# Two-layer GNN with expert FFNs: second FFN product per expert in node order, gate weights applied to its sums

## The reference, cut to what matters

```python
x = x + gnn0(ln(x))   # mean over edges of feat[src] * w, next to feat itself, @ W.T + b
x = x + ffn0(ln(x))   # 8 experts, 256 -> 512 -> 256, relu
x = x + gnn1(ln(x))   # h = relu(x @ Wp.T + bp); h @ W1.T + sqrt(sum over edges of w * h[src]**2) @ W2.T
x = x + ffn1(ln(x))   # 8 experts, 256 -> 256 -> 256, gelu, plus its own input
# both ffn: for every token the two best experts by gate, weights comb[token, e] (0 for the others)
h = act(tokens @ W1[e] + b1[e]); y = h @ W2[e] + b2[e]
out += comb[:, e:e+1] * y        # over all 8 experts
```

## Time and profile before

| | |
|---|---|
| median of 3 runs | 3251.39 us (3250.32 to 3257.69) |
| the profiled execution | 3246.49 us, its span 3244.1 us |
| PE, DVE, ACT, POOL busy | 76%, 55%, 35%, 52% of the span |
| granted PE clock, mean | 0.894 of full speed |
| layer 0, full tile with gathers (tile 8) | 129.9 us |
| layer 1, full tile with gathers (tile 8) | 101.5 us |

### The profile page before, as it was taken

One profiled execution on the slowest core, in us unless ns is written; L12 is line 12 of the kernel. 1 busy time (PEld: TensorE's weight loads), 2 busy tenths in 40 slices (PEclk: granted clock), 3 DMA queues, 4 the chain that ended last, 5 costly groups with the idle time before them and its releaser, 6 DMA issues.

```text
span 3244.1 us, 47395 instructions
## 1 busy us (share of the span) xinstructions
PE 2453.5 (76%) x17987; PEld 1405.7 (43%) x17987; DVE 1779.2 (55%) x4298; ACT 1133.1 (35%) x1835; POOL 1681.3 (52%) x1678
## 2 busy tenths in 40 slices
PE   0136889989989989899999623478787777877897
PEld 0123444544444445444457522344443444444455
DVE  8454666656566566565666433244454544545565
ACT  3022333343343433333545401133232333333455
POOL 3666545454464554544330166566666666666520
PEclk9998999999999999999999855588787888888899
DMA  5532223232232322322220212112212222122110
GB/s 205 202 89 85 80 86 90 81 92 75 85 90 80 92 83 81 89 82 78 68 58 18 81 47 54 41 54 61 59 51 55 62 60 62 51 55 60 50 36 9
DMA packets 115789, 238.02 MB, mean 73 GB/s; under 512 B 30290, under 2 KB 69452, under 8 KB 115044
## 3 DMA queue, kind: packets, MB, share of 16 engines
q0 software_dynamic: 66560, 163.68, 18.2%
q1 hardware_dynamic: 48996, 71.26, 6.4%
HBM read 209.16 MB, written 25.67 MB: 72 GB/s over the span
## 4 chain that ended last, share of the span: by engine, by line
PE 45%; DVE 19%; another core or an unknown queue 16%; issue 12%; ACT 6%; DMA 1%; POOL 1%; DVEq 0%; ACTq 0%; SPq 0%; POOLq 0%
PE psY L714 16%; PE psH L684 14%; DVE hid L1271 4%; PE psM L778 4%; PE psE L674 4%; DVE hsc L1276 3%; PE psE L666 3%; ACT hid L1459 2%; PE psC L691 1%; DVE acc L1110 1%; ACT hsc L1466 1%; DVE wbuf L1022 1%; PE psM L730 1%; DVE mag L968 1%
## 5 line engine op out<-in xcount | busy, mean ns | idle before, releaser
L591 POOL DMA_INDIRECT ring<-table,src_s x1664 | 1653.2, 993 | 1364.3 <-issue 624.9
L714 PE MATMUL psY<-hsc,wbuf 128*128 128x512 f16 (+2 forms) x4032 | 945.3, 371 | 231.7 <-DVE hsc L1276 91.7
L684 PE MATMUL psH<-xnT,wbuf 128*128 128x512 f16 (+2 forms) x4032 | 932.2, 369 | 40.4 <-ACT hid L1459 26.1
L1459 ACT ACTIVATE hid<-psH,b,scl 128x512 f32<-128x512 f32 (+2 forms) x672 | 485.8, 723 | 1289.8 <-PE psH L684 778.5
L1271 DVE TENSOR_TENSOR hid<-hid,psC 128x512 f32<-128x512 f32 (+2 forms) x672 | 415.9, 619 | 573.2 <-ACT hid L1459 408.7
L714 PEld LDWEIGHTS psY<-hsc,wbuf 128*128 128x128 f16 x4032 | 365.2, 101 | 725.6 <-DVE hsc L1276 187.5
L684 PEld LDWEIGHTS psH<-xnT,wbuf 128*128 128x128 f16 x4032 | 383.8, 104 | 373.1 <-issue 79.5
L1110 DVE TENSOR_TENSOR acc<-acc,psE 128x120 f32 (+1 forms) x416 | 98.5, 237 | 656.2 <-remote 477.5
L1276 DVE TENSOR_TENSOR hsc<-hid,hsc 128x512 f16<-128x512 f32 (+2 forms) x672 | 416.3, 619 | 0.4 <-ACT hsc L1466 0.4
L1466 ACT ACTIVATE hsc<-hid 128x512 f16<-128x512 f32 (+2 forms) x672 | 380.1, 566 | 2.9 <-DVE hid L1271 1.9
L674 PEld LDWEIGHTS psE<-ohbuf,ring 128*128 128x128 f32 x1664 | 263.6, 232 | 55.3 <-DMA ring<-table,src_s 22.5
(11 more groups left out here) (155 smaller groups left out, 1764.8 us busy)
## 6 DMA issues: line engine op xcount, KB each, us to landing
ring<-table,src_s POOLq DMA_INDIRECT x1664
wbuf<-w_in SPq DMA_DIRECT2D x2, 4096.0 KB, 16.0
wbuf<-x_in SPq DMA_DIRECT2D x7, 896.0 KB, 11.5
table<-ring SPq DMA_DIRECT2D x7, 896.0 KB, 3.6
feat<-table SPq DMA_DIRECT2D x11, 512.0 KB
xin<-x_in SPq DMA_DIRECT2D x11, 512.0 KB
x_d<-x SPq DMA_DIRECT2D x11, 512.0 KB
xin<-x_d SPq DMA_DIRECT2D x11, 512.0 KB
```

Of the source, the lines that this page charges most:

```text
L591: pool.indirect_dma_start(out=l.ring[:, g % l.R, k, :], out_offset=None, in_=l.table, in_offset=bass.IndirectOffsetOnAxis(ap=src_s[:, c:c ...
L684: last = mm(psH[n % 2][:, 0:l.TT[t]], l.w1(e, i, k, c), x[:, j, k, 0:l.TT[t]], start=(k == 0 and m == 0), stop=(k == KD - 1 and m == 2))
L714: last = mm(psY[d][:, 0:l.TT[t]], l.w2(e, i, c, d), hsc[n % 2][:, j, 0:l.TT[t]], start=False, stop=(n == l.M - 1 and m == 2))
L1459: f(hid[n % 4][:, 0:l.TT[t]], psH[n % 2][:, 0:l.TT[t]], (ACT.Relu, ACT.Gelu)[l.i], scale=l.un_up, bias=l.b1[:, n // l.HC, n % l.HC:n % l.H ...
```

## The change

`down` now takes 128 nodes of the hidden tile as the stationary operand and a 128 x 256 piece of the second matrix as the moving one, so that psY holds nodes by features, four blocks in two banks, for one expert at a time. The bias of the expert comes first, as a product with a matrix that has ones in row e (`spread[:, e, :]`), 24 x 128 by 24 x 256. After an expert's last chunk DVE multiplies each block with its gate weight and adds it to `res`, which is the result at the end of the tile (`weighted`; three `res` tiles in place of two and x2). `scale`, `spread_weights`, `back_to_tokens`, the cut, transposed and copied weights, `sum_copied`, yT, x2 and bank psC are gone. psE has two banks, one for even and one for odd groups; PE may start a group when the one before the last has been added, and DVE adds each group when it alone is summed. In layer 0 the node counts of a group are summed ahead of the wait for its gather. The order by step changes in layer 1 (take, linear, norm, gate at 4, 6, 10, 12; groups from step 5 on, over 15 steps), and the end of `gate_weights` runs in the first steps of the tile that it is for. `t0nb` is made by four operations of one column.

```diff
-                self.at_take, self.at_lin, self.at_norm, self.at_gate, self.at_comb = (
-                    (13, 18, 22, 24, 29), (1, 3, 7, 9, 13))[i]
+                self.at_take, self.at_lin, self.at_norm, self.at_gate = (
+                    (13, 18, 22, 24), (4, 6, 10, 12))[i]
...
-                self.turn = (18, 1)[i]
+                self.turn = (18, 5)[i]
...
+            def window(self, g):
+                o = g % self.OB // 2 * self.parts * W
+                return psE[g % 2][:, o:o + self.parts * W]
...
+            def y(self, s):
+                return psY[s // 2][:, s % 2 * D:(s % 2 + 1) * D]
...
+            def added(self, t, e, b):
+                return NX * self.CB[t] + e * self.NB[t] + b + 1
...
-                    if gs[0]:
-                        pe.wait_ge(l.window_added, gs[0])
+                    if gs[0] > 1:
+                        pe.wait_ge(l.window_added, gs[0] - 1)
...
             def down(l, t, n):
...
+                e, c, b = n // l.HC, n % l.HC, l.BT[t]
+                x, gs = hsc[n % 2], l.at(t, n)
+                if c == 0:
+                    for s in range(b):
+                        if s % 2 == 0 and (e or t):
+                            pe.wait_ge(l.y_added, l.added(t, e - 1, s // 2) if e else NX * l.CB[t])
+                        mm(l.y(s), spread[:, e, :], b2s[l.i][:, :], start=(s % 2 == 0), stop=False)
+                for s in range(b):
+                    v = slice(s * P, (s + 1) * P)
+                    for j in range(2):
+                        if s == 0 and j == 0:
+                            pe.wait_ge(l.hid_hi, l.M * t + n + 1)
+                        if s == 0 and j == 1 and l.i == 1 and n == l.at_lin and t < l.NT - 1:
+                            pe.wait_ge(l.logits_taken, t + 1)
+                        if s == b - 1 and j == 1 and gs and gs[0] > 1:
+                            pe.wait_ge(l.window_added, gs[0] - 1)
+                        mm(l.y(s), x[:, 0, v], l.w2(e, j, c), start=False, stop=False)
+                for s in range(b):
+                    v = slice(s * P, (s + 1) * P)
+                    if s == 0:
+                        pe.wait_ge(l.hid_lo, l.M * t + n + 1)
+                    if s == b - 1 and gs and l.i == 1:
+                        pe.wait_ge(l.onehot_ready, gs[-1] + 1)
+                    last = mm(l.y(s), x[:, 1, v], l.w2(e, 0, c), start=False,
+                              stop=(c == l.HC - 1 and (s % 2 == 1 or s == b - 1)))
                 last.then_inc(l.hid_used, 1)
...
-                dve.scalar_tensor_tensor(t0nb[:, v], t0mv[:, v, 0], -1.0, t0rs[:, v], ALU.mult, ALU.mult)\
-                   .then_inc(s_t0r, 1)
+                for j in range(i * XR, i * XR + XA):
+                    last = ts_(t0nb[:, j:j + 1], t0mv[:, j, 0:1], t0rs[:, j:j + 1], -1.0, ALU.mult, ALU.mult)
+                last.then_inc(s_t0r, 1)
...
-                    dve.wait_ge(l.group_summed, gs[-1] + 1)
+                    dve.wait_ge(l.group_summed, g + 1)
...
+            def weighted(l, t, e):
+                dve.wait_ge(l.hid_used, l.M * t + (e + 1) * l.HC)
+                for b in range(l.NB[t]):
+                    if e:
+                        dve.wait_ge(l.y_added, l.added(t, e - 1, b))
+                    for s in range(2 * b, min(2 * b + 2, l.BT[t])):
+                        r = res[t % 3][:, s, :]
+                        last = dve.scalar_tensor_tensor(r, l.y(s), comb[t % 2][:, s, e:e + 1], r, ALU.mult, ALU.add)
+                    last.then_inc(l.y_added, 1)
...
                     for n in range(l.M):
-                        if n + 1 < l.M:
-                            scale(l, t, n + 1)
-                        elif not last:
-                            scale(l, t + 1, 0)
                         hidden_low(l, t, n)
+                        if n == l.HC:
+                            for _ in weighing:
+                                pass
+                        if n and n % l.HC == 0:
+                            weighted(l, t, n // l.HC - 1)
+                        if n == 0 and t:
+                            result(l, t - 1)
                         add_windows(l, l.at(t, n - 1))
                         onehots(l, l.at(t, n + 1))
```

More of the change, by code:

```diff
@@ L191, in build_program @@
         featT = sb("featT", [P, KD, T])
-        res = [sb(f"res{i}", [P, SUB, D]) for i in range(2)]
+        res = [sb(f"res{i}", [P, SUB, D]) for i in range(3)]
         xn = sb("xn", [P, SUB, D])
@@ L795, in logits @@
                 last.then_inc(l.logits_summed, 1)
-            def weights_transposed(l, u):
-                pe.wait_ge(l.comb_split, u + 1)
-                for s in range(l.BT[u]):
-                    last = pe.transpose(cps[0:CP * NX, s, :], c72[:, s, :], ident_b[:, :])
-                last.then_inc(l.combT_summed, 1)
             for l in L:
@@ L1279, in result @@
-            def result(l, tt):
-                wait(dve, l.out_stored, 16 * tt)
-                for b in range(l.NB[tt]):
-                    dve.wait_ge(l.ytok_summed, l.CB[tt] + b + 1)
-                    v = slice(2 * b, min(2 * b + 2, l.BT[tt]))
-                    tt_(x2[:, v, :], res[tt % 2][:, v, :],
-                        psM[b][:, 0:(v.stop - v.start) * D].rearrange("p (s d) -> p s d", d=D), ALU.add)\
-                        .then_inc(l.out_ready, 1)
+                v = slice(0, l.TT[t])
```

222 lines of the change are left out of this document (69 added, 153 removed).

## The result

| | before | after |
|---|---|---|
| median of 4 runs | 3254.3 us | 3369.6 us (3358.6 to 3380.9) |
| ratio | 1 | 1.036, 95% interval 1.033 to 1.039 |
| span of the profiled execution | 3244.1 us | 3356.8 us |
| layer 0, tiles 8 and 10 | 129.9, 103.2 us | 135.4, 114.3 us |
| layer 1, tiles 8 and 10 | 101.5, 55.7 us | 107.6, 72.5 us |

What follows compares the result with a forecast made beforehand. Layer 0 was taken as PE-bound, layer 1 as a mixture of POOL's gathers and holes. Terms -11 + 16 - 65 - 125 - 12 + 34 + 25 = -138, with 15 held back -123, gave 3128 us, range 3070 to 3190.

Steps and rivals of the forecast that it cites:

- front: Stage ahead of the gathers: four one-column `t0nb` operations end ACT's 13.1 us of waits, passed on whole, -11 us.
- PE's own work: PE in both layers: more second and bias products, less spreading and transposing, +16 us, all on PE's path.
- layer 0 waits: PE's waits in layer 0 for low half, gate weights and spread ones: -55, with clock -10, together -65 us.
- layer 1 waits: PE's waits in layer 1 for gate weights, window sums, low half, spreading product: -110, with the clock -125 us.
- the 15 held back: 15 us kept off the predicted gain for work that moves to tile starts, where gate weights' operations queue on DVE.
- heads and tails: First and last tiles of each layer: gate weights, copies and transposes leave the path, -3 and -3 per layer, -12 us.
- drain: PE waits at each expert's bias product until DVE takes the last sums from psY: +34 layer 0, +25 layer 1.
- Waits that go: Step on PE's waits, heads and tails: shorter chain before the second product, 1.4 us before 2.6 of cover; -65, -125, -12.
- Layer 1 doesn't move: Rival, 0.14: 13.75 us hole stays, gather ring fills behind it, only front and layer 0 count: 3202 us.
- My bound of 181 us: Layer 1: POOL stood 181 us waiting for others than itself; more than that can't be gained there.
- The drain of psY decides, and it is slower: Rival, 0.15: at each expert's first bias product PE loses 1.2 us, 235 us in place of 59: 3304 us.
- loads don't hide: Rival, 0.05: second product's stationary slices of `hsc` load visibly, 0.02 us for each of 3024 more, +60: 3188 us.

Runs made afterwards that it cites:

- late batch: Runs on one chip in one stretch of time, in which the kernel before took 3250 to 3260 us.
- split alone: Kernel before with only the small operation of the first layer norm (`t0nb`) split: 2843.5 against 2846.3 us, ratio 0.999.
- three banks: Changed kernel, psY given the group sums' bank, DVE draining first, PE bank by bank, norm behind drain: 2830.0 us (0.996) prompt, 3266.3 us (1.002) late.
- prompt batches: Runs on one chip in one stretch of time, in which the kernel before took 2841 to 2846 us.
- no drain: Changed kernel, but PE waits for psY and DVE takes it only once a tile: 3235.5 us (0.992) late, 2835.4 us (0.998) prompt.
- b0: Kernel before, unedited and profiled, in a late batch: 3265.9 us.
- b1: Kernel before, unedited, run for its trace in a prompt batch: 2845.1 us.
- the stops: POOL waits until rows land, every group in layer 0, every fourth in layer 1: kernel before 3190.0 us (1.121), three banks 3169.8 us (1.113), prompt.

## Why the prediction was wrong, point by point

The terms against what the runs give, for a late batch, us:

| term | predicted | measured | from |
|---|---|---|---|
| front | -11 | -3 | split alone |
| PE's own work | +16 | about as said | layer 0 tile 113.5 before, 114.6 with three banks, in prompt batches; 0.8 predicted |
| layer 0 waits | -65 | about -26 | an estimate: tiles 1 to 8 take 131.6 before, 129.8 without the drain; 0.8 of own work added back, by ten tiles |
| layer 1 waits | -125 | none | tiles 1 to 8: 102.5 before, 103.9 without the drain |
| all but the drain, after the 15 held back | -182 | -24 | no drain, 0.992 |
| heads and tails | -12 | about -23 | layer 0's last tile and the stage behind it 291.1 to 265.0, layer 1's tile 0 97.3 to 100.1, which also holds the groups moved into it |
| drain | +59 | +161 | changed kernel less no drain, same batch |

"Before" in the tile rows is b0, from the other late batch. -24 and +161 make the +137 us of their batch by the way they were measured; the rows above the -24 are estimates and leave some 12 us of it open.

**The step that failed first is "Waits that go", above all its -125 for layer 1.** It took the listed reasons as the causes, and booked each wait of PE as a gain once its operation was shorter or nearer. The operations were seldom too slow to hide: in a prompt batch, with the same durations (activation 0.78 us, high copy 0.62, low half 0.69), the kernel before loses 14.0 us to the low half in layer 0 where a late one loses 40 to 46. What makes the rest of the holes in a late batch is that ACT, DVE and POOL get PE's updates late, 134 times by 2.0 us in the mean for ACT alone, and the new order's 1.2 us of slack (2.6 of cover for 1.4 of chain) doesn't cover that: without the drain PE stands 45.5 us in layer 0 for the two halves, where I had left 5 for them. Layer 1 tiles are 102.5 us before, 103.9 without the drain, 100 to 108 with three banks, and POOL stands there as long as before (185 us against 181). The 25 us for less time at 1.2 GHz went the other way, too: the mean granted clock fell from 0.894 to 0.877 without the drain. *Layer 1 doesn't move* was right about layer 1, at 0.14; its own reason, one long hole behind which the ring fills, is not what these traces show. The page of the profile had the hint: 16% of the chain that ended last was put down to another core or an unknown queue, and of POOL's stand in layer 1 the largest part beside its own issue time, 129.7 us, was "remote". My bound of 181 us from that row took it for waits that PE could shorten.

**The second is the price of the drain**, 161 instead of 59. *The drain of psY decides, and it is slower* had the mechanism, at 0.15, and a time of 3304, too low because the other terms weren't there; its 1.2 us a boundary is near the dearer ones without a norm (1.15), but the cost isn't spread as it said: half of what a layer 0 tile loses undisturbed is one boundary.
Three things were off. First the times behind a boundary without a group, 0.75 us predicted and 1.35 in the one shown. There the high copy ends 0.28 us behind the old products where I had 0.1 (it takes 0.71 us with its scale from memory where the row said 0.62), the low half takes 0.75 instead of 0.69, DVE's four operations follow each other 0.39 apart instead of 0.35 and start later, so that the second bank is taken at 2.76 us instead of 2.3, and the next products start 0.1 us behind the last bias product. Second, a group between the products pays for less than I had, and more seldom: 0, 0.4 and 0.4 us are left at such boundaries of tile 8, undisturbed, where I had 0.1, and they are three of eight, where I took 17 of 27. Third and largest, I looked only at the operation directly ahead of the drain on DVE, not at what its queue holds at that step: behind the norm of the last result one boundary in eight costs 4.2 us undisturbed, and 5.2 and 7.0 in tiles 10 and 8 of the late trace. I had a bound of 2.0 for a pair of one-hot operations ahead, and the norm exceeds it.
How much of the price the late hand-overs add is not shown: 145 us in a prompt batch (with the group sums in one bank) and 161 in a late one are close.

**The front** failed on where the lock goes. The small operations run at 0.20 us (I had said 0.15 to 0.2), and ACT stands 2.4 us for them instead of 13.1, but POOL's subtraction holds the first of the three normalisations of DVE behind them instead (3.72 us for the three, 1.05 without), and DVE, not ACT, closes the round. I had written that the gain passes on whole.
The Trainium skill ("SBUF — State Buffer", "SBUF: two separate sides"), on which I leaned for one-input forms being free, is borne out by the 0.20 us operations and not by the normalisations: those too read one tensor, with two scalars per partition, and the longest of them took 3.08 us where the median is 0.40, from 41.55 us to 44.63, when POOL's subtraction had ended at 44.48. I had read the Trainium skill's sentence too widely: beside the operations with two SBUF inputs it names those in a 2-port perf mode as ones that wait. Whether the normalisations run in such a mode, no run here shows.

**Right:** PE's own work, and not by luck. Products of 256 columns go at 0.109 us, with a different stationary operand each (eight of L712 are issued in 0.87 us), so *loads don't hide* is out; removed work at the tails shows in the prompt batch (tile 12 of layer 0 takes 55.5 us before, 51.2 with three banks). The bias and the additional products together cost 1.1 us in such a tile, 114.6 against 113.5 in prompt batches.
By the Trainium skill's figure ("TensorE: Matmul & The Clock Gate", back-to-back issue gap), which I had weighed against the change at 76 us in all, the 192 additional products of a full tile of layer 0 would cost an estimated 4.8 us; the traces don't show that.

## What to carry to other kernels

A sum that is taken per expert is a round trip PE - DVE - PE at every expert. Price it from the last product to the second bank, with everything that DVE's program holds ahead of it at that very step. Then move the drain to the front of DVE's queue, which brought most here (late, 1.043 to 1.016 together with PE's order, to 1.010 with the norm behind it), and give the accumulator one more bank than it fills (1.010 to 1.002 from one late batch to another; 0.996 in a prompt one). And before a wait is booked as a gain, ask whether its releaser was done in time: where the profile gives part of the chain to no engine at all, shorter work bought little of it here.

## What I had not expected of the hardware

The same program takes 2842 or 3255 us, by the batch, with the same durations of its operations (above) and of the gathers (1.28 us each in the earlier trace rows, 68 of them in 87.5 us in b1's tile of layer 1). In the slower kind a quarter of PE's semaphore updates reach ACT more than 0.2 us late, in the example DVE and POOL with it, while what ACT and DVE pass on is never late in these counts. It happens where POOL gathers; tiles without gathers are the same in both (layer 0, tile 12: 55.5 us and 55.5). With the holes comes a lower clock of PE: 1.00 in b1's tile 8 of layer 0, where the earlier trace rows had 0.96, and 0.94 against 0.84 in the layer 1 tiles shown.
In the example the updates arrived when POOL stood still with a full ring, and in the prompt batches none is late. Whether POOL's issuing holds them back was to be tested by the stops, which fell on a prompt batch: it stays open, and so does what makes a batch of one kind or the other.
